# Handing the rotation its operands earlier: the shuffle of queries and keys waits for the sine products alone, one product moves ahead of the last masks, and two pieces of GpSimd work change their place

## The reference

```python
q = split_heads(x @ Wq); k = split_heads(x @ Wk); v = split_heads(x @ Wv)
def apply_rope(x):
    x1, x2 = (x[..., 0::2], x[..., 1::2])
    rot = jnp.stack([x1 * cos - x2 * sin, x1 * sin + x2 * cos], axis=-1)
    return rot.reshape(x.shape)
q = apply_rope(q); k = apply_rope(k)
sim = jnp.einsum('bid,bjd->bij', q, k) * scale
sim = jnp.where(causal[None], sim, -jnp.inf)
out = jnp.einsum('bij,bjd->bid', jax.nn.softmax(sim, axis=-1), v)
x = _layernorm(x + out @ Wo + bo)          # heads put side by side again
x = _layernorm(x + ffn(x))                 # 8 experts, the best 2 of each token
```

## Time and profile before

| | |
|---|---|
| time, median of 3 runs | 788.09 us (787.78 to 790.82) |
| time of the profiled execution | 792.1 us |
| its span | 790.3 us |
| PE, DVE, ACT, POOL busy | 96%, 84%, 75%, 72% of the span |
| granted TensorE clock | 0.998 of full speed |

### The profile page before, as it was taken

How to read it: one execution, slowest core, us unless ns; L and a number is a source line. 1 busy time by engine, 2 the same in 40 slices (tenths; PEclk the granted TensorE clock), 3 DMA queues, 4 the chain that set the end, 5 groups by cost and what they waited for, 6 DMA issues and landing times.

```text
span 790.3 us, 20549 instructions
## 1 busy us (share of the span) xinstructions
PE 756.1 (96%) x5763; PEld 534.5 (68%) x5763; DVE 661.1 (84%) x2516; ACT 592.2 (75%) x1678; POOL 572.5 (72%) x699
## 2 busy tenths in 40 slices
PE   8899999999999999999999998999999899999995
PEld 4455666666666666666666665566666589999995
DVE  5888888999899989998998899979988864235997
ACT  3778887888888777878877877778778756565677
POOL 3586767567867966777678868885887167898983
PEclk9999999999999999999999999999999999999999
DMA  4555556565776677565556555655657776424525
GB/s 153 175 173 174 199 182 210 189 225 191 230 212 200 195 199 212 188 207 182 192 194 211 178 174 162 210 178 182 194 189 237 212 202 184 109 79 126 161 89 164
DMA packets 110719, 144.66 MB, mean 183 GB/s; under 512 B 13392, under 2 KB 86352, under 8 KB 110608
## 3 DMA queue, kind: packets, MB, share of 16 engines
q1 hardware_dynamic: 106240, 134.49, 54.4%
q0 software_dynamic: 4224, 8.72, 3.4%
q10 hardware_dynamic: 144, 0.13, 0.1%
HBM read 61.42 MB, written 45.17 MB: 135 GB/s over the span
## 4 chain that ended last, share of the span: by engine, by line
PE 78%; DVE 7%; POOL 6%; issue 4%; DMA 3%; SPq 1%; ACT 0%; DVEq 0%; POOLq 0%
PE AO L1125 17%; PE S_all L1084 16%; PE TB L1105 11%; PE AO L1145 6%; PE S_all L1274 5%; POOL yrows L972 3%; PE AO L1287 2%; PE TB L1287 2%; DVE Sm L1635 2%; POOL shared L989 2%; PE TB L1016 2%; PE AO L1016 1%; PE TB L1014 1%; PE TB L1015 1%; PE AO L1014 1%
## 5 line engine op out<-in xcount | busy, mean ns | idle before, releaser
L1394 ACT ACTIVATE Pr_all<-Sm,nmax 128x512 f32<-128x512 f32 (+3 forms) x512 | 281.8, 563 | 18.5 <-DVE nmax L1635 17.6
L1635 DVE CUSTOM_DVE_ANT_0 Sm<-S_all,causal 128x512 f32<-128x512 f32 (+3 forms) x512 | 222.9, 482 | 46.4 <-PE S_all L1084 45.8
L1084 PE MATMUL S_all<-qk 64*128 64x512 f32 (+3 forms) x1024 | 170.5, 447 | 7.2 <-DVE nmax L1635 5.0
L728 POOL TENSOR_TENSOR qk<-shared,qk 128x512 f32<-128x512 f32 x63 | 81.1, 1287 | 113.0 <-DMA qk<-shared 102.6
L1125 PE MATMUL AO<-PT,shared 128*64 128x128 f32 x1008 | 149.5, 438 | 12.1 <-issue 11.4
L1404 ACT ACTIVATE PT<-TB 128x768 f32<-128x768 f32 x189 | 107.6, 604 | 60.9 <-PE TB L1105 60.9
L1656 DVE SCALAR_TENSOR_TENSOR x_acc<-AO,rinv,x_acc 128x128 f32<-128x128 f32 x504 | 141.7, 344 | 3.6 <-POOL x_acc L782 1.4
L1084 PEld LDWEIGHTS S_all<-qk 64*128 64x128 f32 x1024 | 79.6, 187 | 79.8 <-issue 55.1
L1105 PE MATMUL TB<-ident,Pr_all 128*128 128x128 f32 x764 | 109.2, 279 | 1.1 <-ACT PT L1404 0.6
L1105 PEld LDWEIGHTS TB<-ident,Pr_all 128*128 128x128 f32 x764 | 82.0, 141 | 41.6 <-issue 38.6
L1125 PEld LDWEIGHTS AO<-PT,shared 128*64 128x64 f32 x1008 | 66.1, 136 | 60.3 <-issue 28.0
(11 more groups left out here) (337 smaller groups left out, 1454.0 us busy)
## 6 DMA issues: line engine op xcount, KB each, us to landing
turns<-turned_pr SPq DMA_DIRECT2D x63, 512.0 KB, 2.7
PT<-turns SPq DMA_DIRECT2D x252, 128.0 KB, 3.1
qk<-shared SPq DMA_DIRECT2D x124, 256.0 KB
wo<-in_wo SPq DMA_DIRECT2D x64, 64.0 KB, 3.2
PT<-yrows SPq DMA_DIRECT2D x7, 512.0 KB, 3.9
w_tile<-in_wup SPq DMA_DIRECT2D x10, 256.0 KB
xt<-xrows SPq DMA_DIRECT2D x32, 65.0 KB, 2.0
x_acc<-in_x SPq DMA_DIRECT2D x8, 256.0 KB, 3.3
```

Source lines behind the costliest of these rows:

```text
L728: nc.gpsimd.tensor_tensor(qT[p][:, :], q_cos, qT[p][:, :], ALU.add).then_inc(q_ready, 1)
L1084: nc.tensor.matmul(SB[2 * (group % 2) + h][:, at:at + (qb + 1) * P], qT[p][half, qb * P:qb * P + P], kT[p][half, 0:(qb + 1) * P], start=Tr ...
L1394: nc.scalar.activation(Pr[j][:, 0:n], Sm[j], ACT.Exp, bias=nmax[:, j:j + 1], scale=-1.0, accum_out=rsum[p][:, h * QB + qb:h * QB + qb + 1] ...
L1635: nc.vector.tensor_tensor_reduce(out=Sm[j], in0=SB[2 * (group % 2) + h][:, at:at + n], in1=causal[:, T - n:T], scale=-0.125, scalar=HUGE, ...
```

## The change

The shuffle in SP's `swap` waits for two new semaphores, `q_turned` and `k_turned`, that are raised by the sine products, and no longer for `q_read` and `k_read`, that are raised when both products are made. On POOL the order of the two products was sine, cosine already. On DVE `rope_q` falls into `turn_q` (sine, now first) and `keep_q` (cosine), and `turn_q` stands ahead of the last two masks. The rotations, which read the cosine products, wait for `q_read` and `k_read` themselves. Each buffer stays single. `sum_front`, a piece of POOL's routing arithmetic, moves from unit 45 to 46, and `add_bias` of batches 1 to 7 from the first unit of the batch to the last unit of the batch before (n = 7), behind the row that is sent there. The list `y_last_in` is made two entries shorter.

```diff
-SUMS_AT, REST_AT, NEXT_AT = FRONT_AT + 5, FRONT_AT + PAIRS, FRONT_AT + PAIRS + 1
+SUMS_AT, REST_AT, NEXT_AT = FRONT_AT + 6, FRONT_AT + PAIRS, FRONT_AT + PAIRS + 1
-BIAS_AT = 0
+BIAS_AT = 7
...
+        q_turned, k_turned = sem("q_turned"), sem("k_turned")
...
             def swap(u, p):
-                sp.wait_ge(k_read, u + 1)
-                sp.wait_ge(q_read, u + 1)
+                sp.wait_ge(k_turned, u + 1 - PLAIN)
+                sp.wait_ge(q_turned, u + 1)
...
             def rotate_q(u, p):
                 pool.wait_ge(swapped, SWAPPED * (2 * u + 1 if u < PLAIN else u + PLAIN + 1))
+                pool.wait_ge(q_read, u + 1)
...
             def turn_k(u):
-                nc.gpsimd.tensor_tensor(k_rot, k_cos[u % 2], sin_t[:, :], ALU.mult)
+                nc.gpsimd.tensor_tensor(k_rot, k_cos[u % 2], sin_t[:, :], ALU.mult).then_inc(k_turned, 1)
...
             def rotate_k(u, p):
                 pool.wait_ge(swapped, SWAPPED * (u + PLAIN + 1))
+                pool.wait_ge(k_read, u + 1)
...
-                if n == BIAS_AT and batch > 0:
-                    add_bias(batch)
...
+                if n == BIAS_AT and not last_batch(batch):
+                    add_bias(batch + 1)
...
+            def turn_q(u):
                 dve.wait_ge(q_proj, u + 1)
                 wait(dve, q_ready, u)
-                bank = q_bank(u)
-                nc.vector.tensor_tensor(q_cos, bank[:, :], cos_t[:, :], ALU.mult)
-                nc.vector.tensor_tensor(q_rot, bank[:, :], sin_t[:, :], ALU.mult).then_inc(q_read, 1)
+                nc.vector.tensor_tensor(q_rot, q_bank(u)[:, :], sin_t[:, :], ALU.mult).then_inc(q_turned, 1)
+
+            def keep_q(u):
+                nc.vector.tensor_tensor(q_cos, q_bank(u)[:, :], cos_t[:, :], ALU.mult).then_inc(q_read, 1)
...
+                if not first and u + 2 < UNITS:
+                    turn_q(u + 2)
                 for j in range(FIRST_OF[2], BLK):
                     mask_max(u, j)
...
                 if not first and u + 2 < UNITS:
-                    rope_q(u + 2)
+                    keep_q(u + 2)
```

More of the change, by code:

```diff
@@ L409, in build_block @@
         y_in = [sem(f"y_in{i}") for i in range(B - 1)]
-        y_last_in = [sem(f"y_last_in{i}") for i in range(QB)]
+        y_last_in = [sem(f"y_last_in{i}") for i in range(len(PARTS))]
         summed, last_summed, spaced = sem("summed"), sem("last_summed"), sem("spaced")
@@ L1585, in rope_q @@
             def rope_q(u):
+                turn_q(u)
+                keep_q(u)
+            def turn_q(u):
                 dve.wait_ge(q_proj, u + 1)
                 wait(dve, q_ready, u)
-                bank = q_bank(u)
-                nc.vector.tensor_tensor(q_cos, bank[:, :], cos_t[:, :], ALU.mult)
-                nc.vector.tensor_tensor(q_rot, bank[:, :], sin_t[:, :], ALU.mult).then_inc(q_read, 1)
+                nc.vector.tensor_tensor(q_rot, q_bank(u)[:, :], sin_t[:, :], ALU.mult).then_inc(q_turned, 1)
+            def keep_q(u):
+                nc.vector.tensor_tensor(q_cos, q_bank(u)[:, :], cos_t[:, :], ALU.mult).then_inc(q_read, 1)
                 if u < PLAIN:
-                    dve.wait_ge(q_read, u + 1)
+                    dve.wait_ge(q_turned, u + 1)
                     nc.vector.stream_shuffle(qT[u % 2], q_rot, swap).then_inc(swapped, SWAPPED)
@@ L1606, in rotate_both @@
                 dve.wait_ge(swapped, SWAPPED * (u + PLAIN + 1))
+                dve.wait_ge(k_read, u + 1)
+                dve.wait_ge(q_read, u + 1)
                 nc.vector.tensor_tensor(kT[p][:, :], k_cos[p], kT[p][:, :], ALU.add).then_inc(k_ready, 1)
@@ L1884, in attention @@
                         turn(u, h)
+                if u + 1 == PLAIN:
+                    rotate_both(PLAIN, PLAIN % 2)
+                if not first and u + 2 < UNITS:
+                    turn_q(u + 2)
                 for j in range(FIRST_OF[2], BLK):
@@ L1889, in attention @@
                         turn(u, h)
-                if u + 1 == PLAIN:
-                    rotate_both(PLAIN, PLAIN % 2)
                 if not first and u + 2 < UNITS:
-                    rope_q(u + 2)
+                    keep_q(u + 2)
                 if batch > 1 and n == PLACE_AT:
```

## The result

The changed kernel took 799.38 us (median of 4 runs, 796.74 to 801.33) against 788.49 us before on the same chip: a ratio of 1.0131, with an interval from 1.0093 to 1.0168. It is slower by 1.3%. The forecast was 779.1 us, in a range from 773.5 to 785.0. The profiled execution is the fastest of the four (796.74 us, span 794.9), while the one before (792.1 us, span 790.3) was slower than its kernel's median; so the two traces differ by 4.6 us where the medians differ by 10.9.

What follows compares the result with a forecast made beforehand. The prediction took PE, nearly always busy, to bound the kernel, leaving only its waits to win: 8.5 + 2.0 - 0.5 - 0.3 = 9.7 us, lowered by 0.7 to 9.0 off 788.1, hence 779.1 us, range 773.5 to 785.

Steps and rivals of the forecast that it cites:

- a clash of the bias with DVE: Cost: in unit 47 the moved bias could block DVE's small table operations once, up to 1.29 us; set at 0.3 us.
- waits of the scores for masks in units that had none: Sign of being wrong: PE's scores would wait for DVE's masks in units without such waits before; no size given.
- What bounds the kernel: PE is nearly always busy, 756.1 of 790.3 us; only its waits can be won, chiefly 11.4 us ahead of `attend`.
- The shuffle: On SP, the shuffle no longer waits for the cosine products and starts about 1.2 us earlier in each unit.
- The loads: Loads then wait for the store's landing, going 0.44 us earlier, 1.2 in late units; 8.5 us of `attend` waits won.
- DVE's lateness: With POOL earlier, DVE's routing tails are no longer late and PE waits less for masks: 2.0 us, bounds 0 and 4.0.
- The store: Cost: the earlier shuffle's packets delay the landing of the store still moving, 0.1 us in some 50 units; 0.5 us.
- The cover of the last masks: Time between DVE's last masks and PE's next scores shrinks from 1.24 to 0.56 us, with nothing lost.
- The sum: 8.5 + 2.0 - 0.5 - 0.3 = 9.7 us off the profiled 792.1; 9.0 off the median of 788.1.
- the 0.7 us that I took off: Taken off the gain because waits for landings differ from run to run and are likely partly absent in the median.
- The slower one: Rival: the shuffle gets ahead of the store on the wires, loads start 1.2 us later, say 797 us; chance 0.06.
- take the place of the loads: Rival: DVE's slow tails return PE's gains as waits for masks, gain only 3.5 to 5.5 us; chance 0.20.

Runs made afterwards that it cites:

- bias0: The changed kernel with only the bias back in the first unit of each batch: ratio to the kernel before 0.9897, on another chip run 0.9884.
- old_waits: bias0, but the shuffle waits for both products as in the kernel before: 792.71 us, ratio to the kernel before 1.0025.
- after_masks: bias0 with both query products behind the last masks, sine first, the shuffle waiting only for the sine products: 780.60 us, ratio to the kernel before 0.9874.
- bias_gap: The changed kernel with the bias still in n = 7, but behind the two rotations and ahead of POOL's sine product: 780.69 us, ratio to the kernel before 0.9882.
- dummy_write: bias0 plus two unused POOL fills, which only write SBUF, where the changed kernel has the bias: 789.10 us beside 788.17 for bias0.
- bias_first: The changed kernel with the bias in n = 7 ahead of the row that is sent, not behind it: 787.90 us, ratio to the kernel before 0.9963.
- the second group: bias_gap, bias_first, old_waits and after_masks, run on one chip with the kernel before, which took 791.0 us there.
- the first and third group: First: bias0, bias_only (only the bias moved), dummy_read (unused SBUF-reading addition), dummy_write. Third: repeats and minimal (sine first, new waits). Kernel before: 796.0 and 797.6 us.
- bias_gap_again: bias_gap run a second time, on the chip where the kernel before took 797.64 us: 788.73 us, ratio 0.9903.

## Why the prediction was wrong

**The step that failed** is the last of the costs: "I set 0.3 for a clash of the bias with DVE". It measured 18.5 us between the changed kernel and bias0 on one chip. The mechanism was known. The lock had been read off and the earlier trace rows for line 1732, and the bias was named as one that it might touch. Three things were missed. First, I looked for two-operand work of DVE in unit 47 only, with the early table, and not in the tail of every unit with n = 6, which runs on into the head of n = 7: so six of the seven units with a bias (all but unit 7) had a blocked choice, not one, and five of them grew longer than before. Second, the block does not end with one operation. The bias stood behind a send and ahead of two rotations, and with the shuffle earlier, the rotations were ready as the bias ended. DVE was held up three times in a row, 3.5 us in unit 31, where I had priced a single 1.29 at most. Third, PE's stalls of over 3 us in units 31, 47 and 55 were followed by a lower clock, and that added some 2.5 us in unit 31 alone. One of the signs of being wrong that I had named came true: waits of the scores for masks in units that had none, 23, 31, 39 and 55. My 9.7 us were a sum of small certain gains against one cost of low chance; its size was never bounded from above over all the units with n = 7.

**What bounds the kernel:** right. Without the bias in its way, PE's waits ahead of `attend` were what there was to win.

**The shuffle** 1.2 us earlier: right, 9.19 to 7.90 us into the unit. old_waits shows that the new waits are the whole cause of what was won.

**The loads** 0.44 earlier and bound by the store's landing: right (0.47), and 8.5 us of waits gone was close: 9.7 in the changed kernel. Taking the sine product ahead of the masks had no part in it, which I had not seen: after_masks.

**DVE's lateness**, 2.0 us: not confirmed, and its base was misread. I had taken 4.0 us to be waits behind DVE's tails, but 2.1 of the 5.0 us of mask waits stand in unit 1, before there is any tail. Part of the mechanism is in the traces: four DVE operations of the choice are blocked before (1.29, 0.82, 1.14 and 1.15 us) and none in bias0. But PE's waits for masks, which I said would fall, did not. These are bias_gap's waits:

```profile
PE S_all L1087 <- DVE nmax L1646: 7.1, 11, 1.7
PE AO L1128 <- issue: 2.8, 5, 0.8
```

Without unit 1 and the first scores of unit 2, they are 3.4 us against 2.9 before. In bias_gap, attention from unit 2 to unit 63 is 13.3 us shorter than before and the waits ahead of `attend` 8.6 us less. Of the 4.7 us between them, 1.6 are unit 2's, which unit 1 gives back, and 1.5 are unit 49's, where PE no longer waits for the table. The rest no run takes apart.

**The store**, 0.5 us: nothing, its landing stayed at 2.7 us or just under. **The cover of the last masks** held. Only in unit 1, where the rotation of unit 2 now stands ahead of the last masks, does PE wait for them, 1.72 us. That unit is 1.7 us longer; unit 2 is 1.6 us shorter.

**The sum** of 9.7, or 9.0 on the median, is 1.1 to 1.2%. bias0 measured 1.03 and 1.16%, so without the bias the sum was of the right size. That holds for the sum and for its largest term, the loads, not for each term: the 2.0 us of DVE's lateness are not confirmed, and the 0.5 for the store were not paid. No run shows the 0.7 us that I took off for waits for landings that differ from run to run. The lower end of the range was off by as much: 9.9 and 4.0 from 788.1 give 774.2, not 773.5. **The rivals:** none of them was it. The slower one was put on the wires; the lock was only weighed as a cost of one unit. DVE did take the place of the loads, but for the reason of the bias. The chance of 0.05 for slower was far too small for a change that moves an operation of 1.29 us on an engine that I had just seen blocking DVE.

## What to carry to other kernels

A GpSimd operation that reads SBUF can cost far more than its own time: look, in every unit in which it will run, for small vector operations that read SBUF, those with two such operands above all, and count the GpSimd operations that follow without a gap as one block. A good place is where VectorE reads from PSUM and GpSimd waits for someone else: in bias_gap it cost nothing that could be measured. When one change bundles edits with different mechanisms, bound each one's worst case over all its occurrences: here an edit worth 9 us was sunk by one that could gain next to nothing.

## What the runs showed that I had not expected

A VectorE operation can be blocked before the GpSimd operation that blocks it is seen to start. In the changed kernel L1758 begins at 307.04, while POOL is still sending (until 307.72), and lasts 2.05 us to the end of the bias that stands behind the send. In bias0, where the rotation behind the same send is not ready yet, it lasts 0.18 us; with dummy_write it is 0.18 too. In bias_first a TENSOR_SCALAR of 16 columns, with one SBUF tensor and a column of scalars, was blocked for 2.88 us through the send's end and two rotations, so two full tensors are not needed. Why that one was blocked isn't shown.

The unprofiled time of one kernel differed by over 1% from group to group (788.5 to 797.6 us for the kernel before), as much as these edits win or lose, while the ratios held: 1.0131 and 1.0118 for the changed kernel, 0.9897 and 0.9884 for bias0. The traces show where most of that difference sits. The units with n = 4 of batches 2 to 6 last about 10.0 us in the traces of the two kernels of the result and of the second group, and about 11.1 us in those of the first and third group, whatever the kernel, with one exception on either side; in the changed kernel's two traces these five units make 5.3 of the 9.5 us between the spans. In unit 28 of bias_gap_again, the one that I compared, DVE begins to add the output product 1.15 us after it could in bias_gap. What delays it isn't shown.
